# Two bf16 copies of the row maxima move to ScalarE, and TensorE adds the causal mask of the maxima's scores in the first two chunks

## The reference

```
n = layernorm(x)
q, k, v = n @ Wq.T + bq, n @ Wk.T + bk, n @ Wv.T + bv      # 16 heads of 16 features
q, k = rope(q), rope(k)
y = softmax(where(key <= query, q @ k.T / 4, -inf)) @ v
x = x + y @ Wo.T + bo
n = layernorm(x)
h = silu(fp4(n) @ fp4(w_gate).T) * (fp4(n) @ fp4(w_up).T)  # fp4: round to 4-bit floats, a scale per 16 values
out = x + fp4(h) @ fp4(w_down).T                           # width 256 -> 704 -> 256
```

## Time and profile before

| | |
|---|---|
| time, median of 3 runs | 1284.27 us (1283.06 to 1288.6) |
| the profiled execution | 1279.82 us, of which the span is 1278.0 us |
| PE busy | 1202.1 us (94%) |
| DVE busy | 1101.2 us (86%) |
| ACT busy | 755.0 us (59%) |
| POOL busy | 473.6 us (37%) |
| TensorE's granted clock, mean | 0.975 of full speed |

### The profile page before, as it was taken

One profiled execution on the slowest core, in us unless ns is written; L12 is line 12 of the kernel. 1 busy time (PEld: TensorE's weight loads), 2 busy tenths in 40 slices (PEclk: granted clock), 3 DMA queues, 4 the chain that ended last, 5 costly groups with the idle time before them and its releaser, 6 DMA issues.

```text
span 1278.0 us, 40057 instructions
## 1 busy us (share of the span) xinstructions
PE 1202.1 (94%) x16718; PEld 676.2 (53%) x16718; DVE 1101.2 (86%) x2932; ACT 755.0 (59%) x1630; POOL 473.6 (37%) x501
## 2 busy tenths in 40 slices
PE   7678899999999999999999999999999999999876
PEld 6445454554555555455665655545554456454554
DVE  5799898999889989985688999899998998963875
ACT  4356577777555856766565565466754766666311
POOL 2945454562322121204455562312223011232664
PEclk9879899999999999999999999999999999999988
DMA  4745234322121010120334222210111000000000
GB/s 108 176 104 149 71 85 131 86 59 60 29 60 44 20 52 3 35 69 11 88 107 126 77 68 61 53 47 8 52 52 52 19 2 19 2 11 17 22 17 12
DMA packets 79504, 72.40 MB, mean 57 GB/s; under 512 B 25934, under 2 KB 65744, under 8 KB 79312
## 3 DMA queue, kind: packets, MB, share of 16 engines
q1 hardware_dynamic: 76296, 68.76, 20.2%
q10 hardware_dynamic: 3028, 1.09, 0.4%
HBM read 45.07 MB, written 24.35 MB: 54 GB/s over the span
## 4 chain that ended last, share of the span: by engine, by line
PE 59%; DVE 26%; ACT 4%; DMA 4%; POOL 3%; issue 2%; SPq 1%; ACTq 1%; DVEq 0%; POOLq 0%
PE bank L993 11%; PE bank L969 10%; PE bank L1005 10%; PE bank L948 10%; DVE piece_max L1372 10%; DVE bank L1369 8%; PE bank L1124 6%; PE bank L1064 4%; ACT prob L1258 3%; PE bank L1072 2%; PE bank L1115 2%; DMA inverse_sums<-inverse_dram 2%; DVE piece_max L1369 1%; PE bank L1098 1%; DVE c_mem L1459 1%
## 5 line engine op out<-in xcount | busy, mean ns | idle before, releaser
L1258 ACT ACTIVATE prob<-bank 128x512 f32<-128x512 f32 (+3 forms) x1280 | 593.4, 544 | 269.1 <-PE bank L969 142.7
L1372 DVE TENSOR_REDUCE piece_max<-bank 128x1 f32<-128x512 f32 x768 | 488.5, 678 | 11.7 <-PE bank L948 10.7
L969 PE MATMUL bank<-q_mem,k_mem 99*32 99x512 bf16 (+11 forms) x5120 | 385.8, 344 | 11.9 <-DMA q_mem<-max_rows 6.2
L948 PE MATMUL bank<-k_mem,q_mem 96*32 96x512 bf16 (+14 forms) x5120 | 382.5, 345 | 14.2 <-DVE piece_max L1369 6.9
L993 PE MATMUL bank<-prob,V 128*32 128x512 f32 (+3 forms) x2560 | 296.0, 535 | 7.2 <-ACT prob L1258 5.2
L948 PEld LDWEIGHTS bank<-k_mem,q_mem 96*32 96x32 bf16 x5120 | 137.0, 97 | 190.4 <-issue 110.6
L1597 POOL TENSOR_TENSOR c_mem<-c_mem 128x256 f32<-128x256 f32 (+1 forms) x72 | 82.9, 1153 | 400.1 <-DVE c_mem L1471 400.0
L969 PEld LDWEIGHTS bank<-q_mem,k_mem 99*32 99x32 bf16 x5120 | 147.7, 97 | 155.8 <-issue 63.5
L1369 DVE CUSTOM_DVE_ANT_0 bank<-bank,past_keys 128x32 f32<-128x32 f32 (+15 forms) x512 | 208.3, 471 | 1.9 <-PE bank L948 1.7
L993 PEld LDWEIGHTS bank<-prob,V 128*32 128x32 f32 x2560 | 72.2, 110 | 57.3 <-ACT prob L1258 22.1
L974 PE MATMUL bank<-mask_kq,ident_h 128*32 128x96 bf16 (+3 forms) x2048 | 102.4, 201 | 0.0
(11 more groups left out here) (177 smaller groups left out, 1335.5 us busy)
## 6 DMA issues: line engine op xcount, KB each, us to landing
output_dram<-attn SPq DMA_DIRECT2D x28, 256.0 KB, 3.1
parts_dram<-a_mem SPq DMA_DIRECT2D x13, 512.0 KB, 3.9
q_mem<-parts_dram SPq DMA_DIRECT2D x32, 192.0 KB, 3.1
k_mem<-parts_dram SPq DMA_DIRECT2D x32, 192.0 KB, 3.6
q_mem<-parts_dram SPq DMA_DIRECT2D x32, 128.0 KB, 3.2
k_mem<-parts_dram SPq DMA_DIRECT2D x32, 128.0 KB, 3.6
c_mem<-in_L_attn_x SPq DMA_DIRECT2D x29, 128.0 KB, 2.1
out<-c_mem SPq DMA_DIRECT2D x29, 128.0 KB, 1.7
```

Of the source, the lines that this page charges most:

```text
L948: m = pe.matmul(b[COLUMNS * h:COLUMNS * (h + 1), of], q_rows(u)[0:TERM_ROWS, h, block * COLUMNS:(block + 1) * COLUMNS], k_rows(k0 // CHUNK ...
L969: mm = pe.matmul(b[k0:k0 + COLUMNS, since:CHUNK], k_rows(j // TPC, g)[:, h, first:first + COLUMNS], q_rows(u)[:, h, since:CHUNK], start=Tr ...
L1258: act.activation(prob[:, n % NP, off:CHUNK], bank_of("st", n)[:, off:CHUNK], ACT.Exp, scale=SCALE).then_inc(drained("st", n)[0], 1)
L1372: r = dve.tensor_reduce(most, scores, AX.X, ALU.max)
```

## The change

Three edits. (1) The two casts neg1 and neg3 become ScalarE copies in a new function `round_maxima`; VectorE's neg2 and neg4 wait for them. (2) For units of the first two chunks, TensorE adds the mask to the own parts: behind the four score matmuls come four of the identity against `mask_qk`, a bf16 copy of the 32 x 32 mask of each head, on the last 32 columns; VectorE then uses plain `tensor_reduce`. ScalarE makes `mask_qk` once, and SyncE's load of the feed-forward weights, the first pass and the second pass wait for it as the third constant. (3) The plan is told of this, with the price of own parts that stay on VectorE raised from 66 to 114 ns a part plus 1.045 ns a key, and two of `SOONER_NS` changed: the first pass is due 400 ns early and not 200, the product with v 600 ns late and not 1000.

```diff
@@ -46,7 +46,7 @@
-SOONER_NS = dict(a=0, w=-20000, xn=10000, s=200, st=0, pv=-1000, place=10000, norm=200, c=(0, -2000), tile=1000)
+SOONER_NS = dict(a=0, w=-20000, xn=10000, s=400, st=0, pv=-600, place=10000, norm=200, c=(0, -2000), tile=1000)
@@ -220,6 +220,11 @@
+    def masked_on_tensor(u):
+        return units[u][0] < 2
@@ -372,8 +377,10 @@
-            yield from plan.through(("s1", n), 0.428 * keys, "dve", 66 * len(parts) + 1.04 * keys, [],
-                                    [("mask load", 0)], divided=True)
+            on_tensor = own and masked_on_tensor(u)
+            ns = 114 * len(parts) + 1.045 * keys if own and not on_tensor else 66 * len(parts) + 1.04 * keys
+            yield from plan.through(("s1", n), 0.428 * keys + 40 * len(parts) * on_tensor, "dve", ns,
+                                    [("masks",)] if on_tensor else [], [("mask load", 0)], divided=True)
@@ -385,8 +392,8 @@
-            yield from plan.step("dve", (f"neg{n}", u), 90 if n < 5 else 160, [(f"neg{n - 1}", u)] + (old if n == 5 else []),
-                                 shares=n < 5)
+            engine, ns = ("act", 200) if n in (1, 3) else ("dve", 90 if n < 5 else 160)
+            yield from plan.step(engine, (f"neg{n}", u), ns, [(f"neg{n - 1}", u)] + (old if n == 5 else []), shares=n in (2, 4))
@@ -542,7 +549,7 @@
-    plan.do("act", ("masks",), 215, [("mask load", 1)])
+    plan.do("act", ("masks",), 350, [("mask load", 0), ("mask load", 1)])
@@ -668,7 +676,7 @@
-        MAX_STEPS = 6
+        MAX_STEPS, MAX_ROUNDINGS = 4, 2
@@ -942,13 +951,19 @@
                         of = slice(column, column + keys)
+                        on_tensor = own and masked_on_tensor(u)
                         if own:
                             at.wait_ge(k_dealt[g], 16 * len(RUNS) * (k + 1))
+                        if on_tensor:
+                            at.wait_ge(constants_made, 3)
                         for h in range(GROUP):
...
                                           k_rows(k0 // CHUNK, g)[0:TERM_ROWS, h, k0 % CHUNK:k0 % CHUNK + keys],
-                                          start=True, stop=True)
+                                          start=True, stop=not on_tensor)
+                        for h in range(GROUP if on_tensor else 0):
+                            m = pe.matmul(b[COLUMNS * h:COLUMNS * (h + 1), of.stop - COLUMNS:of.stop],
+                                          ident_h[:, 0:COLUMNS], mask_qk[:, :], start=False, stop=True)
                     m.then_inc(filled("s1", n)[0], 1)
@@ -1180,6 +1195,8 @@
+                at.wait_ge(mask_loaded[0], 16 * GROUP)
+                act.activation(mask_qk[:, :], past_keys[:, BANK - COLUMNS:BANK], ACT.Copy).then_inc(constants_made, 1)
@@ -1257,6 +1274,15 @@
+            def round_maxima(u):
+                yield when["neg1", u]
+                at.wait_ge(max_vector[u % 2], MAX_STEPS * (u // 2) + 1)
+                act.activation(max_parts[:, u % 2, 0, :, 0], neg_max[:, u % 2], ACT.Copy).then_inc(max_scalar[u % 2], 1)
+                yield when["neg3", u]
+                at.wait_ge(max_vector[u % 2], MAX_STEPS * (u // 2) + 2)
+                act.activation(max_parts[:, u % 2, 0, :, 1], neg_rest[:, u % 2], ACT.Copy).then_inc(max_scalar[u % 2], 1)
@@ -1363,7 +1390,7 @@
-                        if own:
+                        if own and not masked_on_tensor(u):
@@ -1376,25 +1403,20 @@
                 done, first = max_vector[u % 2], MAX_STEPS * (u // 2)
+                rounded, before = max_scalar[u % 2], MAX_ROUNDINGS * (u // 2)
                 high, middle, low = (max_parts[:, u % 2, p // 2, :, p % 2] for p in range(SPLIT))
...
                 dve.tensor_reduce(whole, piece_max[:, u % 2, :, 0:c + 1], AX.X, ALU.max, negate=True).then_inc(done, 1)
-                yield when["neg1", u]
-                at.wait_ge(done, first + 1)
-                dve.tensor_copy(high, whole).then_inc(done, 1)
                 yield when["neg2", u]
-                at.wait_ge(done, first + 2)
+                at.wait_ge(rounded, before + 1)
                 dve.tensor_tensor(rest, whole, high, ALU.subtract).then_inc(done, 1)
-                yield when["neg3", u]
-                at.wait_ge(done, first + 3)
-                dve.tensor_copy(middle, rest).then_inc(done, 1)
                 yield when["neg4", u]
-                at.wait_ge(done, first + 4)
+                at.wait_ge(rounded, before + 2)
                 dve.tensor_tensor(low, rest, middle, ALU.subtract).then_inc(done, 1)
                 yield when["neg5", u]
-                at.wait_ge(done, first + 5)
+                at.wait_ge(done, first + 3)
                 at.wait_ge(ones_made, 3)
```

More of the change, by code:

```diff
@@ L577, in preln_layer @@
         mask_kq = sb("mask_kq", [P, P], BF16)
+        mask_qk = sb("mask_qk", [P, COLUMNS], BF16)
         cos_t = sb("cos_t", [P, TILES, HD // 2])
@@ L718, in preln_layer @@
         max_vector = [sem(f"max{s}_vector") for s in range(2)]
+        max_scalar = [sem(f"max{s}_scalar") for s in range(2)]
         project_moments = [sem(f"project{s}_moments") for s in range(len(A))]
@@ L809, in weights @@
                     if n == 0:
-                        at.wait_ge(constants_made, 2)
+                        at.wait_ge(constants_made, 3)
                         for s in range(len(attention_weights)):
@@ L1315, in scalar_engine @@
                     load(("v bias load",), v_bias[:, :], bv.partition_broadcast(P), v_bias_loaded),
-                    biases(), constants(), probabilities(), outputs(), *(attention_weight(s) for s in range(len(attention_weights))),
+                    biases(), constants(), probabilities(), outputs(),
+                    *(round_maxima(u) for u in range(len(units))), *(attention_weight(s) for s in range(len(attention_weights))),
                     *(ffn_weight(n) for n in range(len(ffn_weights))), *(project(z) for z in range(len(pairs))),
```

## The result

The changed kernel takes 1270.38 us (median of 4 runs, 1268.76 to 1279.34), the kernel before beside it 1286.43 us (4 runs). The ratio of the two is 0.9897 with a 95% interval of 0.9864 to 0.9930: 1.0% faster, 9 to 17 us. Forecast were 1275.3 us, 9 us faster.

What follows compares the result with a forecast made beforehand. TensorE leads with VectorE close behind, but VectorE bounds two early stretches. Gains 2.4 - 2.0 + 4.0 + 2.1 + 1.5 + 1.0 = 9.0 us gave 1270.8, plus 4.5 to the median: 1275.3 us, range 1263 to 1290.

Steps and rivals of the forecast that it cites:

- third rival: VectorE-full stretches (52.0-73.5, 121.5-133.8 us) dissolve; half of idle TensorE and slow clock go: 1267.9 us, chance 0.16.
- Masks: Own parts of the first two chunks: 2.4 us gained on VectorE, 2.0 us lost on TensorE.
- TensorE's side: Mask matmuls in the first two chunks: 0.04 us per group, 38.5% on the chain, 2.0 us lost (0.7 to 10.8).
- this reading: Mask matmul overheads paid one after another: 0.10 us a part, 4.9 us lost instead of 2.0; not adopted.
- VectorE's relief: Plain instead of masked reductions in the first two chunks: 2.4 us gained (0 to 6.4).
- Casts: VectorE casts moved to ScalarE: 4.0 us gained in the first eight units, 2.1 us in the other 24.
- Order: Replanned order of all engines and banks: 1.0 us gained (-7 to +5).
- Clock: TensorE's reduced-clock work costs 7.4 us; a fifth comes back, 1.5 us gained (0 to 4).
- The wait for GpSimd: First rival: VectorE's subtractions inherit the casts' GpSimd wait; 1282.3 us, no measurable difference, chance 0.26.
- VectorE's wait for ScalarE: Second rival: VectorE held by late ScalarE copies, 8.6 us lost, 1292.9 us, chance 0.20; sign: wait below 10 us.
- a change of over 6 us behind 205 us: Sign of a wrong prediction: stretch behind 205 us changes over 6 us either way, so order, not moved work, decides.

Runs made afterwards that it cites:

- experiments 9 to 12: Changed kernel's order: 9, masks moved only, 0.9947; 10, casts moved only, 0.9895; 11, second chunk's masks back on VectorE, 0.9906; 12, changed kernel again, 0.9909.
- experiment 7: Changed kernel in its order, with TensorE adding each of the 128 masks twice: ratio 0.9949 to the kernel before, 5.5 us slower than the changed kernel.
- experiment 6: Kernel before with the changed kernel's order and banks only, casts and masks still on VectorE: ratio 0.9954, 5.9 us faster.
- experiments 1 and 2: Kernel before, each newly planned: 1, only the casts moved to ScalarE, 1.0070; 2, only the first two chunks' masks moved to TensorE, 1.0098.
- experiment 3: Kernel before with no instruction changed, only the plan's own-part prices and two due times new: ratio 1.0196, 25 us slower.
- experiment 8: Changed kernel with the old due times and so another order: ratio 1.0015 to the kernel before, 14 us slower than the changed kernel.
- experiment 5: All the moved work, against the kernel before, in that kernel's order and banks: ratio 0.9964, 4.6 us faster.
- experiments 4 and 12: The changed kernel unaltered, measured again beside other experiments: ratios 0.9913 (4) and 0.9909 (12) to the kernel before.

## Why the prediction was right, and where it was right by chance

The time lay 4.9 us below the forecast and inside the range, on the forecast's side. It lay nearer to the third rival's 1267.9 us, by 2.5 us. The gain of 12 us lies between the 9.0 us of the forecast and the 16.4 us of that rival, nearer to the forecast. The total is in part luck: the order brought about half of it, and it was given 1.0 us. By its steps:

*Masks.* Net 0.4 us was forecast, and experiments 9 to 12 find nothing measurable. The net was right by luck if, as the runs suggest, both of its terms were too small. In the record, VectorE does the first ten own parts in 56.26 - 52.95 = 3.31 us:

```profile
52.95 3.39 DVE L1399 TENSOR_REDUCE piece_max<-bank 128x1 f32<-128x32 f32 x10
56.26 1.21 DVE L1545 TENSOR_TENSOR k_mem<-k_mem 128x1024 bf16<-128x1024 f32 x1
```

and the kernel before in 56.28 - 52.51 = 3.77 us:

```profile
52.51 0.19 DVE L1369 CUSTOM_DVE_ANT_0 bank<-bank,past_keys 128x32 f32<-128x32 f32 x1
...
56.28 2.74 DVE L1523 TENSOR_TENSOR k_mem<-k_mem 128x1024 bf16<-128x1024 f32 x1
```

0.046 us a part, close to the 0.052 taken, about 6 us for 128. TensorE's side, measured by experiment 7, costs 5.5 us (2 to 9), nearer its whole 3.8 than 38.5% of it. If that holds for the first set of mask matmuls as for the second, VectorE's relief must be worth about as much, and not the forecast 2.4 us; that step is argued, not measured by itself. The rule of the Trainium skill, "TensorEngine Tiling (Array Packing)", section "Instruction Overhead", would have made a group 0.10 us if the overheads of its four matmuls were paid one after the other. The step of 0.02 to 0.03 us shows that for column tiles side by side they are not: the four together take about one overhead of 60 cycles, an estimated 0.025 us by that page's figure at 2.4 GHz. The 4.9 us that this reading put on the end of the kernel are near what experiment 7 measured, but by another way: the group is cheap and, it seems, counts fully.

*Casts.* 4.0 + 2.1 = 6.1 us forecast, 5.3 and 7.6 measured. The size is right, by two errors that offset each other: I had counted 21.3 us of record and let less than a third of it reach the end. In the new order there were 12.1 to 14.7 us to take, 7.0 to 9.6 us of VectorE's time, and half to all of that came out. Both this and the mask matmuls say that the 26 to 38% by which I priced a line was too low here. My reading, which no run separates: the chain is one path; a small step between a unit's maximum and its second pass has TensorE's next work behind it whether or not the path runs through it.

*Order.* The step that failed: **+1.0 us, at most 5**. It is 5.9 us with the old work and 7.5 with the new, half of the gain or more; both figures are above my bound of 5, though with their 3 to 4 us of uncertainty they can't be put above it for certain. The reason that I gave, that TensorE idles only 5.8 us from 205 to 610 us and so a better order finds little, looked for the gain in the wrong stretch: TensorE's work left behind 141 us is already 5.3 us less in experiment 6. For a loss it was the right stretch: in experiments 1 and 2 TensorE idles 10.8 and 12.9 us there. The other bound was worse still. I allowed a loss of 7 us, and experiment 3 shows 25; experiment 8, set against experiment 5 with the same work, shows 6.5. Nor did the truer prices make the order good: experiment 3 has them and both new due times. Of the five plans drawn anew here (experiments 1, 2, 3, 8 and the changed kernel's) one gave a better order than the old one. So the order's part of the gain is a lucky draw, as far as these runs show.

*Clock.* 1.5 us forecast; by the windows of the earlier trace rows and after, the cost in the same three stretches is now 11.24 x 0.34 = 3.8 and not 7.4 us, 3.6 us less. In those three stretches the order alone does it (9.72 x 0.35 = 3.4 us in experiment 6), but most of it comes back behind them. The same product, added up over thirteen short windows that together cover 52 to 205 us, is 10.0 us before, 9.4 with the order alone (experiment 6), 6.8 with the work alone (experiment 5) and 5.1 in the changed kernel; 7.9 and 5.3 in its profiles of experiments 4 and 12. So the clock came back mostly with the moved work, by 2 to 5 us, and differs by nearly 3 us from one execution to the next.

*The rivals.* The wait for GpSimd did not stay as a whole: the subtractions' means fell. In unit 0 it did, as the chain shows in order of time:

```profile
61.14 0.59 DVE neg_rest L1414
...
64.13 1.23 DVE max_parts L1417
```

The second ends just when GpSimd's instruction of 63.09 + 2.25 = 65.34 us is over, at 65.36:

```profile
63.09 2.25 POOL L1374 TENSOR_TENSOR a_mem<-a_mem 128x512 f32<-128x512 f32 x1
64.13 1.23 DVE L1417 TENSOR_TENSOR max_parts<-neg_rest,max_parts 128x16 bf16<-128x16 f32 x1
```

Both subtractions there wait, 0.59 and 1.23 us on the chain, where the casts had 0.69 and 1.37. So the rule of the Trainium skill, "VectorE: DVE Perf Modes", section "Two Vector instructions with no wait between them", that a two-input operation shares an interface with GpSimd, agrees with this trace, but as a mechanism for the whole it was worth little. VectorE's wait for ScalarE came to 5.3 us, under the 10 named, not the 51 us of that rival. The third rival came nearer than its 0.16 allowed. It let half of the 18.5 us of idle TensorE and half of the 7.4 us of slow clock go; 8.2 us of the idle time and 3.6 us of the slow clock went in those stretches. Its reason, VectorE's relief alone, was only half of it: with the moved work alone (experiment 5) the second stretch keeps 4.3 us of idle TensorE. Among what would show the prediction wrong I had named a change of over 6 us behind 205 us. To the letter it came: the time from there to the end went from 1073.0 to 1062.6 us. But whatever is gained earlier shows there as well, so the sign could not tell the order from the moved work.

## What to carry to other kernels

Where a planner draws the order, an edit has two prices, and they must be measured apart: the new work in the old order, and the old work in the new order. Here each was worth about half a per cent, while each edit with a plan of its own cost 0.7 to 2.0%, and a judgement by those runs would have thrown away a change that gains 1%. After a change of the work, try several due times before it is judged: the old ones cost 14 us here. And the share that a line has in the chain is a weak price: here lines priced at 26 to 38% gave about half to all of their time, the casts when taken away and the mask matmuls when doubled. A window at a fixed time can show a slow stretch as gone that has only moved.

## What the runs showed of the hardware

A group of four 32-column matmuls in four column tiles, each with its own weight load, costs TensorE 0.02 to 0.03 us from start to start at full clock, though each shows 0.19 us from start to end; behind its scores at a granted clock of 0.50 it takes 0.07 us. Nothing else was unexpected: VectorE's cast of 16 values waits for a GpSimd instruction under way, and so does its subtraction (65.34 and 65.36 us above), and a ScalarE copy of 16 values takes 0.233 us, where one of 4 values from PSUM took 0.182.
